# Graph attention with pre-norm on one core: separate loop bounds for TensorE and ScalarE, the third group's normalised rows by way of DRAM, and first scores with a wait per third

## The reference

```python
h = maximum(layernorm(x), 0)                       # per row, 384 wide
q, k, v = h @ Wq + bq, h @ Wk + bk, h @ Wv + bv    # 12 heads of 32
scores = q k^T / sqrt(32) + beta * adj             # per head, 128 x 128
scores = where(adj > 0, scores, -9e15)
out = x + softmax(scores) @ v
```

## Time and profile before

| what | value |
|---|---|
| median of three runs | 520.21 us |
| the profiled execution's own time | 523.37 us |
| its span | 521.5 us |
| TensorE matmul busy | 498.0 us (96%) |
| VectorE, ScalarE busy | 437.5 (84%), 453.1 (87%) us |
| GpSimd busy | 172.2 us (33%) |
| mean granted TensorE clock | 0.997 of full |
| chain that ended last, by engine | PE 66%, DMA 9%, SyncE's queue 9%, ACT 3%, DVE 3% |
| DMA | 106.29 MB, mean 204 GB/s |

### The profile page before, as it was taken

One profiled execution on the slowest core, in us unless ns is written; L12 is line 12 of the kernel. 1 busy time (PEld: TensorE's weight loads), 2 busy tenths in 40 slices (PEclk: granted clock), 3 DMA queues, 4 the chain that ended last, 5 costly groups with the idle time before them and its releaser, 6 DMA issues.

```text
span 521.5 us, 17127 instructions
## 1 busy us (share of the span) xinstructions
PE 498.0 (96%) x5142; PEld 416.2 (80%) x5142; DVE 437.5 (84%) x2250; ACT 453.1 (87%) x1831; POOL 172.2 (33%) x262
## 2 busy tenths in 40 slices
PE   8979999998989989999999999999999989999995
PEld 7758788887868878888888888888888878888774
DVE  5679789988978889888989898898989988766796
ACT  3558898998887889998999999999998998999795
POOL 5422043233332333343244324433423332222131
PEclk9999999999999999999999999999999999999999
DMA  7624568577675868787786868678676666554321
GB/s 227 207 56 157 174 202 260 176 257 230 187 247 169 263 216 248 242 250 249 222 250 220 261 215 255 217 239 249 201 241 211 211 202 201 174 170 160 112 77 47
DMA packets 111967, 106.29 MB, mean 204 GB/s; under 512 B 12448, under 2 KB 97312, under 8 KB 111904
## 3 DMA queue, kind: packets, MB, share of 16 engines
q1 hardware_dynamic: 111904, 105.56, 64.2%
HBM read 55.84 MB, written 49.68 MB: 202 GB/s over the span
## 4 chain that ended last, share of the span: by engine, by line
PE 66%; DMA 9%; SPq 9%; ACT 3%; DVE 3%; issue 3%; DVEq 0%
PE G_ps L907 28%; PE S_ps L974 14%; DMA probs_rows<-probs_blocks 8%; PE S_ps L926 8%; PE PT_ps L958 8%; PE PT_ps L942 7%; SPq L424 4%; SPq L445 2%; ACT probs L560 2%; SPq L400 2%; DVE probs L752 1%; PE G_ps L958 1%; SPq L392 0%; SPq L449 0%; ACT probsT L583 0%
## 5 line engine op out<-in xcount | busy, mean ns | idle before, releaser
L752 DVE CUSTOM_DVE_ANT_0 probs<-S_ps,bias 128x128 f32<-128x128 f32 x768 | 167.6, 287 | 52.0 <-PE S_ps L926 51.8
L560 ACT ACTIVATE probs<-probs,negmax 128x128 f32<-128x128 f32 x532 | 206.1, 396 | 0.0
L575 ACT ACTIVATE probs_blocks<-probs,negmax 128x128 f32<-128x128 f32 x236 | 92.1, 391 | 37.0 <-DVE negmax L752 33.1
L907 PE MATMUL G_ps<-h_hi,w_lo 128*128 128x512 f32 x288 | 117.8, 409 | 0.0
L907 PE MATMUL G_ps<-h_hi,w_hi 128*128 128x512 f32 x288 | 117.1, 406 | 0.0
L907 PE MATMUL G_ps<-h_lo,w_hi 128*128 128x512 f32 x288 | 116.5, 404 | 0.0
L560 ACT ACTIVATION_READ_ACCUMULATOR probs<-probs,negmax 128x1 f32 x532 | 104.0, 196 | 0.0
L482 POOL TENSOR_TENSOR var_eps<-meanvar,eps_col 128x1 f32<-128x1 f32 x64 | 13.2, 207 | 227.9 <-DVE meanvar L677 227.7
L506 POOL TENSOR_TENSOR w_raw<-w_raw,rinv 128x384 f32<-128x384 f32 x58 | 53.0, 913 | 82.0 <-issue 41.6
L926 PEld LDWEIGHTS S_ps<-qk 32*128 32x128 f32 x1536 | 49.4, 187 | 33.0 <-issue 31.4
L926 PE MATMUL S_ps<-qk 32*128 32x128 f32 x1536 | 61.4, 289 | 12.6 <-DVE v L772 6.8
(11 more groups left out here) (60 smaller groups left out, 757.6 us busy)
## 6 DMA issues: line engine op xcount, KB each, us to landing
probs_rows<-probs_blocks SPq DMA_DIRECT2D x59, 256.0 KB, 2.6
probs_moved<-probs_rows SPq DMA_DIRECT2D x236, 64.0 KB, 2.1
out_dram<-w_raw SPq DMA_DIRECT2D x63, 192.0 KB, 2.8
x_ring<-in_x_dram SPq DMA_DIRECT2D x61, 192.0 KB, 3.2
w_raw<-out_rows SPq DMA_DIRECT2D x116, 96.0 KB, 2.7
xhat_rows<-xhat_blocks SPq DMA_DIRECT2D x26, 384.0 KB, 2.8
xhat_moved<-xhat_rows SPq DMA_DIRECT2D x104, 96.0 KB, 2.3
out_rows<-xhat SPq DMA_DIRECT2D x15, 384.0 KB, 2.6
```

The costliest lines, as they stand in the source:

```text
L560: last = nc.scalar.activation(p, p, ACT.Exp, bias=negmax[:, e, j * KC + m:j * KC + m + 1], scale=TURN, accum_out=rowsum[:, e, m * HC + j:m ...
L575: last = nc.scalar.activation(blocks[:, j, :, :], probs[:, a, j, 0, :].rearrange("p (c e) -> p c e", c=HC), ACT.Exp, bias=negmax[:, a, j * ...
L752: last = nc.vector.tensor_tensor_reduce(probs[:, a, j, m, :], S_ps[:, j, m * N:(m + 1) * N], bias[(z.par + 1) % 2][:, z.s, :], 1.0, LARGES ...
L907: mm = nc.tensor.matmul(G_ps[:, u % 2, :], pairs[n][0], pairs[n][1], start=(n == 0), stop=(n == len(pairs) - 1))
```

## The change

Four things change together.

- The loop has bounds of its own on two engines: ScalarE's runs over n = 2 to 13, TensorE's over n = 2 to 15. SyncE's and GpSimd's stay at 4 to 11. The body is two groups as before.
- X_GROUPS goes from 2 to 1. The third group (elements 8 to 11) takes the way through DRAM. Its rows are normalised in slots (0,3) and (1,0), so SyncE's write and read for it start in (0,2) and (0,3). VectorE's lists of which rows to normalise, which statistics to take and which masks to prepare are spelled out anew for n = 0 and 1 (`norms`, `late_norms`, `stats`, `masks`). The `order` helper goes away.
- The transpositions that remain in n = 0 go into PT_ps instead of S_ps, in slots 2 and 3 between the two stretches of the projection instead of after them. With that, `scores` no longer waits for `h_lo_stored`, and ScalarE's high part comes ahead of the store of unit 5.
- `scores` at s = 0 waits for five stored units ahead of its first third, and for the sixth only ahead of its last third.

```diff
     FIRST_LOOP, LAST_LOOP = 4, NG - 5
-    X_GROUPS = 2
+    ACT_LOOP, PE_LOOP = (2, NG - 3), (2, NG - 1)
+    X_GROUPS = 1
...
-                self.between = self.A or s == GROUP - 1
+                self.between = s >= 2
...
                     elif n == 0:
-                        self.norms, self.stats = [self.t], [self.t + 1] + [12] * (s == GROUP - 1)
-                    elif n == 1:
-                        self.norms, self.stats = [8 + s, 12 + s], [9 + s, 13 + s] if s < GROUP - 1 else [16]
+                        self.norms = ([4], [6], [7], [8, 9])[s]
+                        self.late_norms = [5] * (s == 0)
+                        self.stats = ([5, 6], [7], [8, 9], [10, 11])[s]
+                        self.masks = ([], [0], [1], [2])[s]
+                    elif n == 1 and s == 0:
+                        self.norms, self.late_norms, self.stats, self.masks = [10, 11], [12], [12, 13], [3]
+                    elif n == 1 and s == 1:
+                        self.masks = [4, 5]
+                self.first_a = self.A and not self.E
...
-            return S_ps[:, 0 if z.A else z.s, 0:D]
+            return PT_ps[:, z.s % 2, 0:D] if z.P else S_ps[:, z.s, 0:D]
...
-        def slots(eng, body):
-            for n in range(-1, FIRST_LOOP):
+        def slots(eng, body, looped=(FIRST_LOOP, LAST_LOOP)):
+            for n in range(-1, looped[0]):
...
@@ SyncE @@
+                first = z.static and z.groups(0) == 0
+                if first:
+                    load_ahead(z)
-                xhat_here = not (z.static and not 1 <= z.groups(0) <= NG - 3)
+                xhat_here = not (z.static and not 0 <= z.groups(0) <= NG - 3)
                 if xhat_here and z.s == 2:
-                    sp.wait_ge(xhat_ready, order(z.count(2) - 1) + 1)
+                    sp.wait_ge(xhat_ready, z.count(2))
                     write_rows(0)
...
@@ ScalarE @@
                 if z.Q:
                     exponentials_ahead(z)
+                if z.X and z.P and z.between:
+                    high_part(z)
                 if z.P:
                     for u in STORE_Q[z.s]:
                         store_qk(z, u)
...
-            slots(act, slot)
+            slots(act, slot, ACT_LOOP)
@@ VectorE, slot @@
-                if z.M:
+                if z.M and not z.first_a:
                     transpose_blocks(z)
-                for q in z.norms[:1]:
+                for q in z.norms:
                     normalise(z, q)
+                if z.first_a:
+                    add_bv(z)
...
+                if z.M and z.first_a:
+                    transpose_blocks(z)
+                for q in z.late_norms:
+                    normalise(z, q)
...
@@ TensorE @@
-                if z.X or z.static and z.t == (X_GROUPS + 1) * GROUP:
-                    pe.wait_ge(h_lo_stored, z.t)
-                if z.s == 0:
-                    pe.wait_ge(qk_stored, z.units(0))
                 for m in range(KC):
+                    if z.s == 0 and m != 1:
+                        pe.wait_ge(qk_stored, z.units(m // 2 - 1))
                     for j in range(HC):
...
             def transpose_xhat(z):
-                pe.wait_ge(xhat_ready, order(z.t) + 1)
-                if z.A:
-                    pe.wait_ge(masked_two, z.a + 1)
-                elif started(z.t - 3):
-                    pe.wait_ge(h_lo_stored, z.t - 3)
+                pe.wait_ge(xhat_ready, z.t + 1)
+                if z.P and z.s >= 2:
+                    pe.wait_ge(h_lo_stored, z.t - 1)
...
                     for part in STRETCH_1[z.s]:
                         project(z, *part)
+                if z.X and z.P and z.between:
+                    transpose_xhat(z)
...
-            slots(pe, slot)
+            slots(pe, slot, PE_LOOP)
```

More of the change, by code:

```diff
@@ L250, in __init__ @@
                     self.t = B
-                self.norms, self.stats = [self.count(2)], [self.count(2) + 1]
+                self.norms, self.late_norms, self.stats, self.masks = [self.count(2)], [], [self.count(2) + 1], [self.count(0)]
                 if self.static:
@@ L358, in slots @@
                         body(Slot(i, off, s))
-            for n in range(LAST_LOOP + 1, NG + 1):
+            for n in range(looped[1] + 1, NG + 1):
                 for s in range(GROUP):
@@ L457, in slot @@
                     sp.dma_start(out[bass.ds(z.o - d, 1), :, :].rearrange("b t d -> t (b d)"), y[:, place, :]).then_inc(out_written[place], 16)
-                load_ahead(z)
+                if not first:
+                    load_ahead(z)
                 if z.L:
@@ L680, in normalise @@
                 s, at = z.place(q)
-                dve.wait_ge(rstd_ready, order(q) + 1)
-                if z.X and q >= GROUP:
+                dve.wait_ge(rstd_ready, q + 1)
+                if GROUP <= q < 2 * GROUP:
                     dve.wait_ge(hT_in_psum, q - 3)
-                if isinstance(q, int) and q < 3 * GROUP:
+                if q < 2 * GROUP:
                     goes, came = xhat[:, s % GROUP, :], x_ring[:, bass.ds(at, D)]
@@ L702, in low_part, with mask_terms, mask_bias @@
                                                op0=ALU.max, op1=ALU.subtract).then_inc(h_lo_stored, 1)
-            def mask_terms(z):
-                if z.s == 0:
[L706 to L711, removed]
-                if z.static and z.groups(0) == 0 and z.s == 0:
+            def mask_terms(q):
+                par, place = q // GROUP % 2, q % GROUP
+                if place == 0:
+                    dve.wait_ge(adj_loaded[par], 16 * (q // (2 * GROUP) + 1))
+                if q > 0:
+                    dve.wait_ge(bias_ready, q)
+                nc.vector.tensor_scalar(mask_term[:, :], adj_in[par][:, place, :], 0.0, TURN * MASKED, ALU.is_le, ALU.mult).then_inc(mask_ready, 1)
+            def mask_bias(q):
+                par, place = q // GROUP % 2, q % GROUP
+                if q == 0:
                     dve.wait_ge(const_loaded, 64)
@@ L715, in mask_bias @@
                     dve.wait_ge(beta_ready, 1)
-                dve.wait_ge(mask_ready, z.count(0) + 1)
-                nc.vector.scalar_tensor_tensor(out=bias[z.par][:, z.s, :], in0=adj_in[z.par][:, z.s, :], scalar=beta_turned[:, 0:1],
+                dve.wait_ge(mask_ready, q + 1)
+                nc.vector.scalar_tensor_tensor(out=bias[par][:, place, :], in0=adj_in[par][:, place, :], scalar=beta_turned[:, 0:1],
                                                in1=mask_term[:, :], op0=ALU.mult, op1=ALU.add).then_inc(bias_ready, 1)
@@ L749, in mask @@
                 dve.wait_ge(scores_in_psum, z.a + 1).then_inc(mask_begun, 1)
-                for j, signal in zip(MASK_ORDER, (masked_one, masked_two, None, masked)):
+                for j, signal in zip(MASK_ORDER, (masked_one, None, None, masked)):
                     for m in range(KC):
@@ L842, in slot @@
                     quotient(z)
-                if z.T and not z.P and z.s > 0 or z.X and z.A and not z.E:
+                if z.T and not z.P and z.s > 0:
                     low_part(z)
@@ L1040, in slot @@
                     transpose_probs(z, 1)
-                if z.X and z.P and z.between:
-                    transpose_xhat(z)
                 if z.E:
```

59 lines of the change are left out of this document (27 added, 32 removed).

## The result

The changed kernel takes 514.38 us (median of four runs, 511.50 to 518.86); beside it the kernel before took 520.67 us (median of four, that is the three of the prediction's 520.21 and one more). The ratio is 0.988, 95% interval 0.983 to 0.992. The forecast was 510.6, its whole range 505.5 to 517.0, its own range 508 to 513: the direction was right, the time lies in the whole range and outside its own, and the gain of 6.3 us is two thirds of the 9.6 of the sum.

What follows compares the result with a forecast made beforehand. TensorE was taken as the bound, with losses in the head, the middle and the end. Head -5.7, middle -4.0, end -1.3, loop cost +0.9 and second wait +0.5 sum to -9.6 from 520.21: 510.6 us, own range 508 to 513, whole 505.5 to 517.

Steps and rivals of the forecast that it cites:

- Part 1: Slot row n = 0: scores start at about 25.7 instead of 27.61, -1.9 us; VectorE's added work put at nothing.
- Part 2: Slot (1,0): waits for row 8 and `add_bv` and one transposition go, 8.45 to 6.3 us, -2.2.
- Part 3: Slots (1,1) to (1,3): low-part waits and three transpositions go, second mask 1 us late, -1.6 us.
- wrong altogether: Sign that the whole forecast fails: VectorE's mask of element 1 being 3 us or more behind the scores.
- Part 4: TensorE's loop from n = 2: SyncE catches up in groups 4 and 5, -4.0 us; the 1.29 at 121.61 stays.
- the slower rival: SyncE never catches up, every start of groups 2 to 6 has a bubble: 524.1 us; chance 0.05.
- Part 5: TensorE's and ScalarE's loops to n = 15 and 13: late code packets mostly go, -1.3 of 2.2 us lost.
- Part 6: Cost of looping: 29.92 against 29.78 us written out, 0.14 more for each of six groups, +0.9 us.
- the two rules of the Trainium skill: Taken branches outside the instruction window force a fetch, so unroll; crossing into the next code block is cheap, mostly hidden.
- Part 7: Second wait in `scores`: wins nothing in the steady state, one more register wait per looped group, +0.5 us.
- The rival at 514.4: VectorE becomes the bound of group 1, so only Part 1 comes in the head: 514.4 us; chance 0.10.

Runs made afterwards that it cites:

- f2: Changed kernel with TensorE's loop cut in two at group 8, making its code new again there: 513.13 us, ratio to before 0.988.
- f5: Kernel before with only `add_bv` put ahead of VectorE's transposition of the probabilities in a group's last slot: 522.61 us, ratio 0.998.
- e2: Changed kernel with only TensorE's last loop bound moved back (n = 2 to 11, written out from 12): 514.13 us, ratio to before 0.988.
- e4: Changed kernel with `add_bv` ahead of VectorE's transposition of the probabilities in a group's last slot: 509.27 us, ratio to before 0.979.
- e1: Changed kernel with TensorE's and ScalarE's loops both back at n = 4 to 11: 518.5 us, ratio to before 0.995.
- g2: e4 with VectorE's mask 3 and one normalisation moved from slot (1,0) to (1,1), masks in pairs behind: 511.27 us, ratio to before 0.976.
- f1: Changed kernel again, nothing altered, for more executions and a second profile: 514.08 us, ratio to before 0.986.
- f3: Changed kernel with SyncE's loop cut in two at group 8, TensorE's left whole: 512.62 us, ratio to before 0.986.
- e3: Kernel before with only longer loops, TensorE's n = 4 to 15 and ScalarE's 4 to 13: 520.6 us, ratio 0.998.
- f6: e4 with a group's first scores waiting once for all units of q and k, as before: 513.82 us, ratio to before 0.980.
- f4: e4 with the loads of x issued one slot earlier: 510.84 us, ratio to before 0.982.

## Why the prediction was right or wrong

**What it rested on stands.** TensorE bounds the loop, q8 is its code, code that is new to it makes the write land late, and the chain by SyncE's queue, VectorE's transposition and `add_bv` gives the bubbles. f2 shows this as cause, which the trace of before showed only as coincidence. Incomplete was the last link: with SyncE over about 5 us late there is a second way to TensorE, by `probs_times_v`, and the late rows of x are a third, by VectorE's statistics (f5, and 2.83 of the waiting in slot (3,3) of after).

**Part 1** (-1.9, scores at 25.7): 25.17, better than said. But TensorE's start is not what the head hangs on. VectorE's first mask went from 29.63 to 28.38, -1.25.

**Part 2** (-2.2): slot (1,0) went from 8.45 to 7.22 in after, 7.66 in f2, 6.75 in e2 and e4: -0.8 to -1.7. Where x came late it was longer than before (9.48 in e1, 9.46 in g2).

**Part 3** (-1.6) failed: 24.56 became 24.15, -0.4 (from VectorE's first mask to group 2 it is 28.16 us where it was 30.99). I had charged one wait of 1.0 us and then let VectorE gain 0.8 a slot. Measured are 8.63, 8.04 and 7.48 us. The mask of element 1 starts 3.21 us behind its scores, 1.9 later than before and not 1.0; this is the sign that I had named for "wrong altogether" (3 us or more), and it was too strict, since it cost this part 1.2 us and not the head. The wait runs by ScalarE's store and exponentials too, and "at nothing" for VectorE's added work in n = 0 (part 1) was wrong, since that work stands ahead of the first mask. Head in all -4.1 where -5.7 was said.

**Part 4** (-4.0): groups 4 and 5 have no q8, the write lands in 2.2 us, and groups that start without a bubble take 29.9, all as said. (In after group 4 still takes 31.47, since it starts at the lower clock.) But "code that is new to it is read for n = 2 and 3 either way, so I leave the 1.29" was wrong: groups 2 and 3 together are 62.7 to 66.9 us in after, f1 and f3, 61.3 in e2 and 60.7 in f2, where before had 60.99. Groups 2 to 5 as a whole, mean of after, f1, e2, f2 and f3, are 123.2 us against 125.9 of before, e3 and f5: -2.7, with single executions from +2.1 to -5.6. The condition of the slower rival (SyncE 2.5 us late before group 2) did not occur: in slot (1,3) of after its load comes 0.44 us behind the scores. But its mechanism did, one group later: 1.66 us behind in (2,0), and 4.10 in (2,1), after the write issued at 62.48 had taken 5.47 us with a q8 packet at 65.27. It recovered once no more code came after group 3. Whether the third group's round trip makes SyncE late, or only TensorE's earlier start against an unchanged queue, no run tells apart.

**Part 5** (-1.3): -2.3 in the profile, where I took six tenths of the 2.2. With TensorE's bound back e2 loses 1.3 of it, and with both back e1 loses 1.1. In the times this part is not resolved (e2, e3).

**Part 6** (+0.9): less. Of the groups that the longer loop takes in, group 12 is at 29.94 and 13 to 15 at about 29.8 us, group 2 of e2 at 29.94: 0.2 in all at the end, 0.16 in that group at the front. The 0.14 between 29.78 and 29.92 goes by VectorE's order and not by the branch: with `add_bv` first, looped groups take 29.82 (178.93 / 6). Slot (5,3) of after, with the branch at its end, takes 7.47 (177.35 to 184.82), as slot (7,3) took 7.48 before. On the two rules of the Trainium skill (Runtime: NRT & Kernel Launch, Instruction fetch mechanics) that the prediction names: there is no stall at a taken branch here, and no q8 packet in the loop either, so code that had to be fetched was never the target, and what a branch to such code costs these runs do not show. And what was mostly hidden for the engine that fetches was not so for others' transfers (writes of 4.3 us in place of 2.2).

**Part 7** (+0.5): nothing that f6 shows.

**The base.** Measured by stretches, the terms come to -4.1 - 2.7 - 0.2 - 2.3 = -9.3, near the sum of -9.6. That is luck in part: the head and the middle gave 2.9 us less than said, the end 1.0 more, and parts 6 and 7 cost next to nothing where I had put 1.4. The medians give 6.3. The rest is that I read the losses in an execution of 523.37 us and subtracted them from a median of 520.21; part of what was there to win belonged to a bad execution. From 523.37 the sum gives 513.8, and f1's profiled execution took 514.14. How much of the 3 us is this and how much chance in the means stays open.

The rival at 514.4 (VectorE the bound of group 1, only part 1 comes) lies nearest by its number and names a true mechanism, but its price was 3.8 us where 1.6 were missing.

## What to carry to other kernels

TensorE's first pass through code is a load on the DMA engines, and the victim is whoever waits for a transfer in an in-order queue; a loop on TensorE pays where such a round trip is tight. On the engine that waits for the round trip, put ahead of that wait whatever the bounding engine needs next, and expect it to help only while the lateness is shorter than the time to the second use, and only if nothing else that waits (here the rows of x) stands ahead of it. Read losses from more than one execution before subtracting them from a median.

## What the runs showed of the hardware

Not expected was the spread. A code packet of 16 KB that begins while a 256 KB write is in flight makes it land in 4.3 us in the median of 72 cases, up to 5.8, where the others take 2.2. In e4 and f6, with packets at 64.38 and 64.39 us, it decided between 2.7 and 5.4 us from the write to the load. Two profiled executions of the changed kernel, 514.14 and 518.86 us, differ by 4.7, and their groups 2 to 5 by 4.8.

The length of an idle time alone does not decide TensorE's clock. After 1.78 us (g2, e1), 2.16 us and 4.02 us (after) its next matmuls ran at the lower of its two levels, in f4 even after 1.29 us (granted clock 0.57 from 27.9 to 31.9 us). After 1.56 us (89.42 in after), 1.83 us (119.17 in f3) and 1.89 us (81.09 in f6) the granted clock stayed at 1.00.
